# Pacing the first group's scattered rows by TensorE's progress, with the order of work searched anew

## The chip, the cores and the metric

The kernel runs on one core of one Trainium2 chip. Its metric is device time in microseconds (us). Each run is one execution of the whole program; the median of three runs of the kernel before is 510.87 us.

## The reference

The input is `x` of 8 batches x 512 tokens x 128 features, float32. Three steps add to it:

```
x = x + 0.5 * ffn(layernorm(x))
x = x + attention(layernorm(x))
x = x + 0.5 * ffn(layernorm(x))
```

`ffn` is a mixture of experts. A shared expert (128 to 2 x 256 to 128, silu(gate) * up) works on every token. Of 8 routed experts of the same size, each token goes to the two with the highest `sigmoid(x @ router.T + bias)`; their outputs are weighted by these scores over their sum. `attention` is linear attention with 8 heads of 16: q and k are rotated by position, k and v are summed over the 512 tokens into a 16 x 16 matrix a head, numerators and denominators come from q, a 5-tap convolution of v is added, the sum is multiplied by a gate and projected. It needs a whole batch at a time; the experts don't care for batches.

## The kernel before

**Tiles.** A batch is 4 tiles of 128 tokens. Routed rows are sorted by expert through DRAM. The batches form groups: (0,2), (2,5), (5,8) in the first `ffn` (called 1), and (0,2), (2,5), (5,7), (7,8) in the second (called 3). For a group, routing computes where each token's two copies go. GpSimd then writes them there by indirect DMAs: one **scatter** moves 128 rows of one tile for one of its two experts, so the first group has 2 x 8 = 16 scatters. SP loads the sorted rows two blocks of 128 at a time (a **pair**), TensorE transposes them, multiplies them by the expert that each block belongs to, and SP stores the result. When all of a group's pairs are stored, GpSimd fetches each token's two results back with indirect DMAs (a **gather**, 128 rows each), and VectorE adds them to `X`. There are 128 scatters and 128 gathers in all.

**Units.** A large product that fills a bank of PSUM is a **unit**: half of a batch's shared expert (S), a routed pair (R), or a third of a batch's attention projections (A). Each has one or two `front` halves. After the first half of a unit TensorE raises the semaphore `half_ready`, after the last `gu_ready`. ScalarE takes silu, VectorE multiplies (`hs`), TensorE multiplies down.

**The opening.** The weights come as float32; ScalarE and VectorE cut each expert's into a high and a low part (`cut_w`, `cut_w_lo`, line 1449 for VectorE) before the first routed pair may start. In the meantime the norms, the shared units of the first `ffn` and the routing of the first groups go on. SP first loads the inputs, then fills the DRAM rooms of the sorted rows with zeros. The first group's scatters need its places, its normalized rows and that fill.

**The order of work.** Every engine's queue is written out by the program `Plan`. It describes about a thousand operations with costs in units of 10 ns, what they need and when their results land. `schedule` simulates them as a list: each engine takes, of the operations that could start within 100 ns of the first, the one with the best rank. `search` runs it 600 times with randomly shifted ranks (seed 1) and keeps the order with the earliest end. The queue orders, the choice of buffers and the semaphore values all come from that one plan.

**The pace of moves.** Scatters and gathers are the **moves**. In `schedule` a move may start no sooner than `PACE` = 160 (1.6 us) after the start of the move before, as long as the last routed unit isn't done. Its own cost is 126. In the program, `pace` lets GpSimd wait before each move for TensorE's progress: `through` counts the unit halves that were finished in the plan when the move started, and GpSimd waits for that value of `half_ready` and `gu_ready`. Both don't hold for the scatters of the first group, which `paced` leaves out:

```
def paced(self, key):
    return key[:3] != ("scatter", *GROUP_LIST[0])
```

GpSimd's queue holds, besides the moves, only the 24 norm roots (`root`, line 1130); a root that stands behind a waiting move waits as well. SP's queue holds the loads, stores and outputs; `load` of a group's first pair waits for all of its scatters.

Of the kernel before, what the change touches and what calls it, by code (L numbers as in the profile page):

```python
# [34 lines left out]
GROUP_LIST = [(l, g) for l in (1, 3) for g in range(NG[l])]  # L35
# [38 lines left out]
class Plan:  # L74
# [275 lines left out]
    def schedule(self, rank):  # L350
        ops, end, start = self.ops, {}, {}
# [21 lines left out]
        def finish(key):  # L373
            for user in users.get(key, ()):
                missing[user] -= 1
                if missing[user] == 0:
                    admit(user)
# [59 lines left out]
        def settle(key, t):  # L437
            name = key[0]
            if name == "front" and (key[2] == 1 or (*key[0:2], 1) not in ops):
                self.units.append(key[1])  # L440
                if key[1][0] in "RS":
                    self.hidden.append(key[1])
            if name in count:
                count[name] += 1
            if name == "hidden_turn":
                ht[0] = ("hT_copy", key[1])
            if name == "sdown":
                ht[0] = ("add", key[1], key[2], "shared")
                self.shared_order.append(key[1:3])
            if name in self.HELD:  # L450
                i = min((i for i in range(2) if not bank[i] or after(bank[i]) is not None),
                        key=lambda i: after(bank[i]) if bank[i] else 0)
                self.misc[key], bank[i] = i, (self.HELD[name], *key[1:])
            if name == "hi":
                i = min((i for i in range(XT) if not xt[i] or after(xt[i]) is not None),
                        key=lambda i: after(xt[i]) if xt[i] else 0)
                l, b = key[1:]
                self.xt_before[l, b] = xt[i] and xt[i][1]
                self.xt_of[l, b] = i
                xt[i] = ("front", ("A", b, "VG") if l == 2 else ("S", l, b, 1), 0)  # L460
            if name == "gather" and key[3] == 0:
                i = min((i for i in range(YG) if not yg[i] or after(yg[i]) is not None),
                        key=lambda i: after(yg[i]) if yg[i] else 0)
                l, b = key[1:3]
                self.yg_before[l, b] = yg[i] and yg[i][1:3]
                self.yg_of[l, b], yg[i] = i, ("add", l, b, "second")
# [4 lines left out]
        last_routed = ("front", ("R", len(self.pair) - 1), 0)  # L471
        while waiting:
            near = {}
            for key in waiting:
                t = dynamic(key)
                if t is None:
                    continue
                engine = ops[key][0]
                t = max(t, ready_at[key], free[engine])
                if key[0] in ("scatter", "gather") and self.paced(key) and last_routed not in end:  # L480
                    t = max(t, last_move + PACE)
                near.setdefault(engine, []).append((t, key))
            best = None
            for engine, candidates in near.items():
                soon = min(t for t, _ in candidates) + NEAR
                t, key = min((c for c in candidates if c[0] <= soon),
                             key=lambda c: rank[c[1]])
                if best is None or t < best[0]:
                    best = (t, serial[key], key, engine, t)
            if not best:  # L490
                return False
            _, _, key, engine, t = best
            waiting.discard(key)
            settle(key, t)
            length = ops[key][1]
            if engine == "PE":
                if t - free[engine] > COLD and t > 1000:
                    cold = t + COLD
                length = length if t >= cold else 1.8 * length
            start[key], end[key] = t, t + length  # L500
            free[engine] = end[key]
            if key[0] in ("scatter", "gather"):
                last_move = t
            self.order[engine].append(key)
            finish(key)
        return True

    def paced(self, key):
        return key[:3] != ("scatter", *GROUP_LIST[0])

    def through(self, key):

        if not self.paced(key):
            return 0, 0
        t = self.start[key]
        return tuple(sum(1 for u in self.units if self.end.get(("front", u, j), t) + HOP <= t) for j in (1, 0))


def build(nc, x, wq, wqp, wk, wv, wg, wo, lepe_w, lepe_b, sgate, sup, sdown, gate_w, up_w, down_w,
# [8 lines left out]
    with ExitStack() as ctx:  # L528
# [596 lines left out]
        def _(pool):  # L1125
# [6 lines left out]
            def pace(*key):  # L1132

                half_through, through = plan.through(key)
                wait(once, half_ready, half_through)
                wait(once, gu_ready, through)
# [424 lines left out]
```

## Time and profile before

| | us |
|---|---|
| median of 3 runs (lowest to highest) | 510.87 (510.63 to 511.22) |
| profiled execution, span from the first to the last instruction | 540.9 |
| TensorE busy in it | 474.9 |
| VectorE busy | 348.5 |
| GpSimd busy | 282.4 |
| ScalarE busy | 272.3 |

The profile is of one execution; the page gives its span and no other time of it. Busy times are of that execution. In the page's second part each digit is the busy share of a fortieth of the span in tenths. In a timeline, the bracket at a line's end is the idle time of the engine before the instruction and what ended it: `issue` is time in which nothing shown was waited for, `remote` an origin outside the engines shown.

### The profile page before, as it was taken

Reading aid. Unit: us, or ns where it says so; the run is one execution under the profiler, and the core shown is the slowest. Engines: PE = TensorE matmul, PEld = TensorE weight load, DVE = VectorE, ACT = ScalarE, POOL = GpSimd, SP = SyncE. Lnnn points to the kernel's source line nnn. Section 1 sums busy time; section 2 is a strip of 40 time slices with the busy share of each in tenths; the row PEclk is TensorE's granted clock in tenths of the full one; section 3 lists DMA queues with packets and bytes.
Section 4 is the critical chain, followed back from the end, with each engine's and each line's share of the span. In section 5 each row is a group of like instructions: output and inputs, shape, how many; then the busy total and the mean of one; then the engine's idle time right before and its main releaser. Section 6 shows DMA issues by size and latency. Waiting matters only on the chain.

```text
span 540.9 us, 9674 instructions
## 1 busy us (share of the span) xinstructions
PE 474.9 (88%) x2975; PEld 381.7 (71%) x2975; DVE 348.5 (64%) x1064; ACT 272.3 (50%) x612; POOL 282.4 (52%) x290
## 2 busy tenths in 40 slices
PE   7894687998999999999999999999999998899980
PEld 3673676776777787777877777877777776667760
DVE  4992795322358765889996789998966224344442
ACT  5861232555566466647647556653554543443530
POOL 4167054545566506666715666776555545553543
PEclk9999799999999999999999999999999999999997
DMA  8961112234431223321132321113442433442222
GB/s 240 377 215 55 54 64 68 79 112 130 121 89 55 87 80 109 103 65 58 57 102 75 86 66 59 45 45 93 121 133 82 127 95 92 124 127 59 79 73 68
DMA packets 74352, 53.66 MB, mean 99 GB/s; under 512 B 9664, under 2 KB 68928, under 8 KB 74304
## 3 DMA queue, kind: packets, MB, share of 16 engines
q1 hardware_dynamic: 66112, 36.26, 22.4%
q0 software_dynamic: 8192, 16.79, 10.0%
q8 instruction: 26, 0.43, 0.3%
q14 instruction: 22, 0.18, 0.1%
HBM read 26.87 MB, written 26.15 MB: 98 GB/s over the span
## 4 chain that ended last, share of the span: by engine, by line
PE 53%; DVE 23%; issue 8%; ACT 7%; another core or an unknown queue 4%; DMA 2%; POOL 1%; SPq 1%; DVEq 0%; POOLq 0%; ACTq 0%
PE gu L881 15%; PE ht_ps L872 7%; PE gu L839 6%; PE gu L841 6%; PE gu L840 5%; PE xt_ps L822 3%; DVE hs L1219 2%; DVE hs L1215 2%; ACT gs L1025 2%; PE gu L799 2%; DVE raw L1415 2%; PE gu L801 1%; PE gu L800 1%; ACT xn L1048 1%
## 5 line engine op out<-in xcount | busy, mean ns | idle before, releaser
L1172 POOL DMA_INDIRECT yg<-y_sorted,places x128 | 123.0, 961 | 113.2 <-PE gu L841 72.4
L1151 POOL DMA_INDIRECT x_sorted<-xn,places x128 | 129.9, 1015 | 97.3 <-PE gu L841 36.2
L881 PEld LDWEIGHTS gu<-w,hT 128*128 128x128 f32 x708 | 87.1, 191 | 36.0 <-issue 33.7
L881 PE MATMUL gu<-w,hT 128*128 x708 | 100.3, 284 | 11.3 <-ACT hT L1031 6.7
L1025 ACT ACTIVATE gs<-gu 128x512 f32<-128x512 f32 x124 | 72.2, 583 | 53.5 <-PE gu L801 19.4
L1215 DVE TENSOR_TENSOR hs<-gs,gu 128x512 f32<-128x512 f32 x92 | 60.7, 662 | 49.6 <-ACT gs L1025 27.0
L839 PE MATMUL gu<-w,xbt_hi 128*128 x177 | 83.6, 473 | 7.1 <-ACT ys L1006 2.9
L1031 ACT ACTIVATE hT<-ht_ps 128x512 f32<-128x512 f32 x92 | 53.3, 580 | 56.6 <-PE ht_ps L872 38.8
L1201 DVE TENSOR_TENSOR xbt_lo<-xt_ps,xbt_hi 128x256 fp32r<-128x256 f32 x92 | 37.7, 410 | 64.9 <-ACT xbt_hi L1014 56.5
L841 PE MATMUL gu<-w,xbt_hi 128*128 x177 | 70.7, 399 | 0.0
L840 PE MATMUL gu<-w,xbt_lo 128*128 x177 | 70.2, 397 | 0.0
L1006 ACT ACTIVATE ys<-gu 128x256 f32<-128x256 f32 x92 | 34.4, 375 | 54.3 <-PE gu L881 41.0
L872 PE MATMUL ht_ps<-squares_sb,hs 128*128 128x128 f32 x354 | 55.5, 278 | 4.6 <-DVE hs L1215 3.5
L872 PEld LDWEIGHTS ht_ps<-squares_sb,hs 128*128 128x128 f32 x354 | 40.9, 141 | 18.7 <-DVE hs L1215 10.7
L1014 ACT ACTIVATE xbt_hi<-xt_ps 128x256 fp32r<-128x256 f32 x92 | 34.4, 373 | 27.8 <-PE gu L841 14.4
L1130 POOL TENSOR_TENSOR rstd<-ve,minus_half 128x4 f32<-128x4 f32 x24 | 26.8, 1116 | 40.0 <-DVE ve L1259 38.4
L1048 ACT ACTIVATE xn<-X,shifts,rstd 128x128 f32<-128x128 f32 x96 | 40.8, 486 | 13.3 <-DVE shifts L1263 10.1
L839 PEld LDWEIGHTS gu<-w,xbt_hi 128*128 128x128 f32 x177 | 33.8, 191 | 15.3 <-issue 13.1
L1238 DVE SCALAR_TENSOR_TENSOR X<-yg,wsel,X 128x128 f32<-128x128 f32 x128 | 36.4, 346 | 7.0 <-DMA yg<-y_sorted,places 6.5
L1219 DVE TENSOR_TENSOR hs<-gs,gu 128x512 f32<-128x512 f32 x32 | 21.8, 682 | 28.1 <-ACT gs L1025 25.7
L841 PEld LDWEIGHTS gu<-w,xbt_hi 128*128 128x128 f32 x177 | 33.6, 190 | 7.8
L822 PE MATMUL xt_ps<-squares_sb,xb 128*128 128x128 f32 x177 | 35.1, 277 | 4.2 <-DVE xbt_lo L1201 2.9
(132 smaller groups left out, 799.4 us busy)
## 6 DMA issues: line engine op xcount, KB each, us to landing
xb<-x_sorted SPq DMA_DIRECT2D x85, 128.0 KB
y_sorted<-ys SPq DMA_DIRECT2D x85, 128.0 KB
x_sorted<-yg SPq DMA_DIRECT2D x6, 512.0 KB, 5.7
X<-x_dram SPq DMA_DIRECT2D x8, 256.0 KB, 4.8
x_sorted<-xn,places POOLq DMA_INDIRECT x128
yg<-y_sorted,places POOLq DMA_INDIRECT x128
out_dram<-X SPq DMA_DIRECT2D x8, 256.0 KB
raw<-gate_w_dram SPq DMA_DIRECT2D x4, 256.0 KB, 4.3
```

What stands on the lines that cost most here:

```text
L822: mm = pe.transpose(xt_ps[:, j * P:(j + 1) * P], xb[r % XB][:, j], ident)
L839: pe.matmul(dst[:, j], xbt_hi[r % 2][:, at], hi, start=True, stop=False)
L840: pe.matmul(dst[:, j], xbt_lo[r % 2][:, at], hi, start=False, stop=False)
L841: mm = pe.matmul(dst[:, j], xbt_hi[r % 2][:, at], lo, start=False, stop=True)
L872: mm = pe.transpose(ht_ps[:, q * P:(q + 1) * P], hs[n % HB][:, q * P:(q + 1) * P], ident)
L881: mm = pe.matmul(dst[:, j * D:(j + 1) * D], hT[r % 2][:, at:at + P], w_flat[:, bass.ds(expert[r][j] + 2 * GU + half * D, D)], start=half = ...
L1025: nc.scalar.activation(dst, src, ACT.Silu).then_inc(silu_done, 1)
L1031: nc.scalar.activation(hT[r % 2][:, 0:n], ht_ps[:, 0:n], ACT.Copy).then_inc(hT_done, 1)
L1048: ins = nc.scalar.activation(xn[:, b, t], X[:, b, t], ACT.Identity, bias=shifts[:, l, b, t:t + 1], scale=rstd[:, l, b, t:t + 1])
L1151: nc.gpsimd.indirect_dma_start(x_sorted[l, g], bass.IndirectOffsetOnAxis(places[l, g][:, k, t:t + 1], 0), xn[:, b, t % T], None).then_inc( ...
L1172: nc.gpsimd.indirect_dma_start(yg[slot][:, k, t], None, y_sorted[l, g], bass.IndirectOffsetOnAxis(places[l, g][:, k, at:at + 1], 0)).then_ ...
L1215: v.tensor_tensor(hs[n % HB][:].rearrange("p (j i) -> p j i", j=2)[:, 0:k], gs[n % GB][:].rearrange("p (j i) -> p j i", j=2)[:, 0:k], bank ...
```

## The change

The exception for the first group is taken out. In the plan its 16 scatters too lie at least 1.6 us after the move before, and in the program GpSimd waits before each of them for TensorE's progress. Since the plan's search runs over the changed rule, the whole order of work, on every engine, may come out another. No operation is added or removed.

```diff
-                if key[0] in ("scatter", "gather") and self.paced(key) and last_routed not in end:
+                if key[0] in ("scatter", "gather") and last_routed not in end:
                     t = max(t, last_move + PACE)
...
-    def paced(self, key):
-        return key[:3] != ("scatter", *GROUP_LIST[0])
-
     def through(self, key):
-
-        if not self.paced(key):
-            return 0, 0
         t = self.start[key]
         return tuple(sum(1 for u in self.units if self.end.get(("front", u, j), t) + HOP <= t) for j in (1, 0))
```

## Rows read from the trace of the kernel before

**Rows 1.** The page: span, busy time of engines, TensorE and its granted clock by slices.

```profile
span 540.9 us, 9674 instructions
...
PE 474.9 (88%) x2975; PEld 381.7 (71%) x2975; DVE 348.5 (64%) x1064; ACT 272.3 (50%) x612; POOL 282.4 (52%) x290
...
PE   7894687998999999999999999999999998899980
...
PEclk9999799999999999999999999999999999999997
```

**Rows 2.** Stretches: length, busy us of each engine (instructions), clock, DMA share, GB/s.

```profile
57.16:78.73 21.57, 19.52 (x124) 16.82 (x124) 20.63 (x61) 6.01 (x13) 6.02 (x6) 0.89 0.17 54
...
57.91:61.89 3.98, 3.98 (x10) 3.13 (x10) 3.67 (x13) 0.80 (x2) 0.00 (x0) 0.51 0.28 81
...
200.00:300.00 100.00, 95.43 (x624) 78.94 (x622) 79.98 (x243) 60.73 (x139) 57.41 (x56) 1.00 0.28 82
300.00:400.00 100.00, 93.49 (x615) 77.88 (x614) 88.84 (x275) 53.72 (x121) 65.51 (x64) 1.00 0.25 75
```

**Rows 3.** Timeline of GpSimd, then of SP: start, us, line, operation, idle before.

```profile
31.89 1.17 POOL L1151 DMA_INDIRECT x_sorted<-xn,places  x1 [0.20 <-issue]
33.10 2.03 POOL L1130 TENSOR_TENSOR rstd<-ve,minus_half 128x4 f32<-128x4 f32 x2
...
53.07 0.96 POOL L1151 DMA_INDIRECT x_sorted<-xn,places  x1 [0.30 <-issue]
69.01 0.96 POOL L1151 DMA_INDIRECT x_sorted<-xn,places  x1 [14.98 <-DVE places L1379]
...
55.32 2.43 SPq L729 DMA_DIRECT2D xb<-x_sorted  x5
...
116.09 3.20 SPq L729 DMA_DIRECT2D xb<-x_sorted  x4
```

**Rows 4.** Timeline of VectorE: the first instruction after each of three waits.

```profile
43.84 0.19 DVE L1280 TENSOR_TENSOR L<-misc,tables_sb 128x32 f32<-128x32 f32 x1 [2.20 <-remote]
...
57.16 0.69 DVE L1219 TENSOR_TENSOR hs<-gs,gu 128x512 f32<-128x512 f32 x1 [10.50 <-ACT gs L1025]
...
89.15 0.17 DVE L1358 TENSOR_SCALAR padded<-misc 128x8 int32<-128x8 f32 x1 [3.45 <-remote]
```

**Rows 5.** Timeline of ScalarE.

```profile
56.53 0.60 ACT L1025 ACTIVATE gs<-gu 128x512 f32<-128x512 f32 x1 [11.42 <-remote]
...
90.58 0.60 ACT L1031 ACTIVATE hT<-ht_ps 128x512 f32<-128x512 f32 x1 [3.86 <-remote]
```

**Rows 6.** Timeline of TensorE: shared units start at L799, transposes of loaded rows at L822.

```profile
41.11 0.48 PE L799 MATMUL gu<-xt_hi,sw_hi 128*128 128x512 f32 x1
...
44.79 0.47 PE L799 MATMUL gu<-xt_hi,sw_hi 128*128 128x512 f32 x1
...
57.91 0.80 PE L799 MATMUL gu<-xt_hi,sw_hi 128*128 128x512 f32 x1 [6.62 <-DVE hs L1219]
...
73.69 0.38 PE L822 MATMUL xt_ps<-squares_sb,xb 128*128 128x128 f32 x2
...
76.70 0.48 PE L799 MATMUL gu<-xt_hi,sw_hi 128*128 128x512 f32 x1
```

**Rows 7.** Waits from 28 to 66 us: us in total, times, longest.

```profile
PE ht_ps L892 <- issue: 2.7, 2, 1.7
```

**Rows 8.** Timeline of GpSimd in the second group's scatters.

```profile
83.45 0.99 POOL L1151 DMA_INDIRECT x_sorted<-xn,places  x1 [1.35 <-PE gu L841]
...
88.53 0.96 POOL L1151 DMA_INDIRECT x_sorted<-xn,places  x1 [0.30 <-issue]
```

**Rows 9.** DMA queues from 40 to 48 us, then from 48 to 56.

```profile
q8 instruction: 1, 0.02, 0.7%
...
q0 software_dynamic: 192, 0.39, 12.4%
```

## The prediction

> **What bounds the kernel now.** I read the page first. Its second part shows TensorE at nine tenths nearly everywhere, with one deep dent in the fourth slice (a slice is 13.5 us), where its granted clock dips as well [rows 1]. The table of stretches gives the rest: TensorE is busy 95.43 of 100 us in the middle of the run and 93.49 in the next hundred [rows 2]. So TensorE bounds all but the opening, and what is gained in the opening is kept, as long as the routed work that follows can start earlier.
>
> GpSimd's timeline says what runs in the dent. The 16 scatters of the first group go out between 31.89 and 54.03 us: one, two norm roots, then 15 in a row, 0.96 us of work and 0.30 us between them [rows 3]. The other three engines' timelines show a hole beside it. VectorE stands 2.20 us before 43.84 and 10.50 us before 57.16 [rows 4]. ScalarE stands 11.42 us before 56.53, and the profile names none of this core's engines as the releaser [rows 5]. TensorE halts twice, 2.7 us together, inside one set of 16 matmuls (L892) that needs nothing new in between [rows 7], and then stands 6.62 us before 57.91 [rows 6]. So the hole is no wait that the program wrote. It starts about 11 us into the run of scatters and ends when the last one has landed: SP's first load of sorted rows, which waits for all 16, goes out at 55.32, ScalarE resumes at 56.53 [rows 3, 5].
>
> Which engine's time in the opening counts is read from the stretch after the hole: from 57.16 to 78.73, where the first routed matmul starts, VectorE is busy 20.63 of 21.57 us [rows 2]. The opening is VectorE's chain (routing of the second group, cutting the expert weights, the shared units), so the hole's price is VectorE's: 2.20 + 10.50 = 12.70 us. The half clock behind the hole (0.51 granted, the 1.2 GHz level, after TensorE had stood for 6.62 us) fits ten matmuls into 3.98 us, where the full clock would need about half of that [rows 2]; VectorE is busy 3.67 of those 3.98 us, so I count it at nothing and keep half, 2.0 us, as the bound.
>
> **The change part by part.**
> (1) The 16 scatters get waits on `half_ready` and `gu_ready`: each starts when TensorE has finished as many units as it had in the plan. Nothing is added to GpSimd's work. A wait already met costs nothing to see: a paced scatter whose wait was met starts 0.30 us after the one before, as an unpaced one does (88.53 and 53.07 [rows 3, 8]).
> (2) In the plan, moves now lie at least 1.6 us apart. 16 scatters then begin over 15 x 1.6 = 24.0 us, where before it was 53.07 - 31.89 = 21.2 us. Of the last one's start to the first load 2.25 us pass (53.07 to 55.32 [rows 3]). So the first load goes out at 31.89 + 24.0 + 2.25 = 58.1 in place of 55.32, if TensorE keeps to the plan. Who waits: SP's queue (five loads stand behind it), then TensorE's first transposes of rows at 73.69 [rows 6]. If the hole's 12.70 us go, these are wanted at 61.0: from 58.1 plus 2 us of landing (estimate: the scatters' own 2.25) that is just in time. So this costs nothing in the likeliest case, with less than one us of cover left; its upper bound is in the third rival.
> (3) Behind a waiting scatter stand the norm roots of later batches (two at 33.10, after the first scatter [rows 3]). A scatter that waited one unit would hold them: two neighbouring units start 3.7 us apart here (41.11 and 44.79 [rows 6]). The plan knows of that order, so I take 0; the bounds are 0 and one such step, 3.7 us.
> (4) What the pace takes away: a burst that runs on while TensorE stands. With it, when TensorE is held, GpSimd stops too. I take it that the long hole goes. It won't go wholly: under the same pace, the second group has five scatters at 1.26 us from 83.45 to 89.5 (TensorE was ahead), and there ScalarE stands 3.86 us and VectorE 3.45 us, again with no releaser named [rows 4, 5, 8]. So I leave one such hole of 3.5 us in the account: 12.7 - 3.5 = 9.2 us gained. Bounds: 12.7 + 2.0 = 14.7 us (all of it and the clock), and 0 (the paced scatters bunch as those did).
> (5) The second group's first scatter starts at 69.01, released by its places [rows 3]; 12.7 us earlier, at 56.3, it would find the first group's last one still out until about 57. That holds 24 scatters back by a us, and their rows are first loaded at 116.09 [rows 3], long after: nothing.
> (6) The order of all work is searched anew, some 600 random trials over the same costs. No row prices another order. Two hundreds of this kernel with the same kind of work differ by 95.43 - 93.49 = 1.9 us of TensorE's idle time [rows 2]; over 4.6 such hundreds, were each to differ at random, about 4 us. I take 0, and 4 us either way as the bound.
>
> **From the profile to the runs.** The sum in the profiled execution: 540.9 - 9.2 = 531.7 us. The page gives that execution its span alone, and it is 30.0 us over the 510.87 us median of the runs. TensorE's idle time in it is 540.9 - 474.9 = 66.0 us [rows 1]. The added 30 us must lie in such idle time for the most part, since matmul steps are at full clock outside the holes (granted 0.98 in the mean). If all of it lies there and evenly, 36/66 = 0.55 of any hole stands in an undisturbed run. So I forecast 0.55 x 9.2 = 5.1 us: **505.8 us**, faster. The ends are 0 (the hole is the profiled execution's alone) and 9.2 (it is whole).
>
> The Trainium skill (Runtime: NRT & Kernel Launch, "Instruction fetch mechanics") says that an engine draws its instructions in blocks through a DMA queue of its own while it works on the block before, mostly unseen. The trace bears that out at the hole: one instruction packet between 40 and 48 us, none between 48 and 56, where the software queue's packets took 12.4% of the DMA engines' time [rows 9]. So neither late instructions nor full DMA engines are the visible cause, and a cause that isn't the burst's would leave the hole where it is: by that the time stays 510.9, the first rival.
>
> **The rivals.**
> *No gain: the hole isn't the scatters' doing, or is mostly the profiled execution's.* For it: no DMA load and no releaser in the hole, and the scatters run for 10 us (from 31.89 to 41.6) before VectorE is held [rows 3, 4, 9]; the 30 us between span and median. Against: the hole ends with the scatters. Worth 0 +/- 4 us from the new order: 510.9, from 507 to 515.
> *Partial bunching.* The plan's units run late on the chip, so the waits are met when reached, and the scatters bunch as at 83.45. Then one or two holes of 3.5 to 7 us stay: 0.55 x (12.7 - 7) = 3.1 us, 507.7. It has the forecast's sign and is part of its range.
> *Slower: the first group's rows come late.* The last scatter may hang on the last shared units. The six shared units left then start from 57.91 to 76.70, 3.8 us apart, at VectorE's pace [rows 6]. Without the hole the last starts at 76.70 - 12.7 = 64.0; a scatter freed at its end, 65.5, is loaded at 67.7 and in at 69.8, and TensorE wanted the rows at 61.0: 8.8 us in which it has no shared unit left to do. That price is real in every run, the hole perhaps not. It decides from the point where the delay is more than what the hole was worth in the runs (0 to 9.2 us). With the hole worth nothing and half the price paid: 510.87 + 4.4 = 515.3 us; with all of it 519.7.
>
> **How the numbers follow.** Forecast with partial bunching 0.45, time 501 to 509.5. No gain 0.23. Late rows 0.32, of which nearly all slower. About 0.2% (1 us) is what a measurement of this kernel can tell from no change. Faster: 0.45 + 0.06 (a lucky order in the second case) = 0.51. Same: 0.12. Slower: 0.05 + 0.32 = 0.37. Range: the low end is 9.2 whole and 1.5 us of luck in the order, 500; the high end takes in the rival's middle, 515.5. As cases of both signs are likely, the forecast's own range is 501 to 509.5.
>
> **What would show it.** Right: in the profile after, the fourth slice of TensorE, VectorE and ScalarE loses its dent, no wait over 4 us without a releaser stands before 60 us, the granted clock stays at full there, the first routed matmul starts near 78.7 - 9.2 = 69.5 us, and later stretches keep their 93 to 95% of TensorE. Step 2 is wrong if TensorE's first transposes of rows wait for the load. Step 4 is wrong if the 16 scatters still run at 1.26 us beside a hole, or run spaced and the hole is there. The third rival shows as waits of GpSimd's first-group scatters on the late shared units, and TensorE idle before its first routed unit. If the profiled span falls by 9 us and the median doesn't, the hole was the profile's.

## The result, and the profile after

The change makes the kernel slower where it was timed: 518.39 us median (518.11 to 519.9, four runs) against 510.75 (510.27 to 511.22, four runs), a ratio of 1.0159 with a 95% interval of 1.0141 to 1.0177. The forecast was 505.8, faster. Ratios here and below compare only fast executions with fast ones on the same chip, so a ratio can differ a little from that of the medians beside it.

One fact has to come first, since no number below can be read without it. The kernel before was timed on six occasions, and its medians fall into two groups. On two of them, the timing of the change among them, it takes 510.6 to 510.8 us. On the four others it takes 538.6 to 542.7, each time on another chip. I speak of 511 chips and 540 chips after that. In the experiments no chip was used on two occasions, so it isn't shown whether the group goes with the chip or with something else about the occasion. The rows ahead of the prediction ([rows 1] to [rows 9]) are from one execution that by its span of 540.9 belongs to the second kind, while the times beside them were from the first kind. The profile after is from a 511 chip. Its execution took 518.11 us at a span of 516.1: recording adds nothing that is seen here, and the two us are what lies around the span.

The page of the changed kernel (busy time, TensorE, VectorE and granted clock by slices of 12.9 us):

```profile
span 516.1 us, 9677 instructions
...
PE 472.0 (91%) x2975; PEld 382.6 (74%) x2975; DVE 348.6 (68%) x1064; ACT 275.2 (53%) x612; POOL 283.4 (55%) x290
...
PE   8899959999999999999999999999999989998980
...
DVE  4999963332678856999995999999875234442442
...
PEclk9999979999999999999999999999999998999996
```

The dent of [rows 1] is gone from slice four, as forecast, and a smaller one stands in slice six (64.5 to 77.4 us), with the dip of the clock. The timelines of the engines in that place, first TensorE (L816 transposes loaded rows, L833 is a routed unit's first product), then VectorE (L1443 cuts an expert's weights, L1195 takes the low part of a loaded pair's rows, L1373 ends a group's routing), then GpSimd and SP:

```profile
63.70 0.38 PE L816 MATMUL xt_ps<-squares_sb,xb 128*128 128x128 f32 x2
...
66.19 2.02 PE L886 MATMUL ht_ps<-swd,hs 128*128 128x128 f32 x16 [2.11 <-DVE X L1222]
...
69.82 0.41 PE L816 MATMUL xt_ps<-squares_sb,xb 128*128 128x128 f32 x2 [0.88 <-DVE xbt_lo L1195]
73.33 0.79 PE L833 MATMUL gu<-w,xbt_hi 128*128 x1 [3.10 <-DVE w L1443]
...
61.26 0.63 DVE L1443 TENSOR_TENSOR w<-raw,w 128x512 fp32r<-128x512 f32 x1
...
67.58 0.41 DVE L1195 TENSOR_TENSOR xbt_lo<-xt_ps,xbt_hi 128x256 fp32r<-128x256 f32 x1
...
69.26 0.41 DVE L1195 TENSOR_TENSOR xbt_lo<-xt_ps,xbt_hi 128x256 fp32r<-128x256 f32 x1
...
72.42 0.18 DVE L1373 CAST places<-spot_f 128x24 int32<-128x24 f32 x1
72.51 0.69 DVE L1443 TENSOR_TENSOR w<-raw,w 128x512 fp32r<-128x512 f32 x1
...
32.47 1.17 POOL L1145 DMA_INDIRECT x_sorted<-xn,places  x1 [13.18 <-PE gu L795]
...
58.81 1.29 POOL L1145 DMA_INDIRECT x_sorted<-xn,places  x1 [0.30 <-issue]
...
61.39 9.23 SPq L723 DMA_DIRECT2D xb<-x_sorted  x8
```

The reader is to see three things. The first group's last scatter starts at 58.81 and the first load goes out at 61.39. The rows are in, and TensorE transposes them from 63.70 on. The first routed product still starts only at 73.33, and what it waits for last, for 3.10 us, is the last expert's weights: VectorE cuts them at 72.51, directly behind the end of the third group's routing at 72.42. TensorE stands 2.11 and 0.88 us before that as well, each time for VectorE. Nothing asks for that routing so early: the third group's scatters start at 105 us. The order is the plan's. Later stretches are as full as [rows 2] or fuller (columns as there; those of the old plan on a 511 chip, in `waits_only_2` below, are fuller still, with TensorE at 97.04 and 96.64):

```profile
200.00:300.00 100.00, 96.66 (x649) 80.69 (x648) 89.64 (x285) 63.91 (x146) 59.67 (x59) 1.00 0.28 80
300.00:400.00 100.00, 96.27 (x619) 79.89 (x618) 85.58 (x265) 54.59 (x122) 66.23 (x65) 1.00 0.28 86
```

### The profile page after: what moved, and what is told of

Same layout as the page of the kernel before. It is cut to its first block, busy times and chain, and to the rows that moved or that the text cites. A ratio compares the mean times of both kernels' runs of the same rounds, so it can differ in the third digit from the quotient of the medians.

```text
span 516.1 us, 9677 instructions
## 1 busy us (share of the span) xinstructions
PE 472.0 (91%) x2975; PEld 382.6 (74%) x2975; DVE 348.6 (68%) x1064; ACT 275.2 (53%) x612; POOL 283.4 (55%) x290
## 4 chain that ended last, share of the span: by engine, by line
PE 59%; DVE 24%; issue 7%; ACT 5%; POOL 2%; DMA 2%; SPq 1%; POOLq 0%; DVEq 0%; ACTq 0%
PE gu L875 16%; PE gu L833 8%; PE ht_ps L866 8%; PE gu L835 7%; PE gu L834 7%; PE xt_ps L816 3%; DVE hs L1213 3%; PE gu L793 2%; PE gu L795 2%; PE gu L794 2%; DVE hs L1209 2%; DVE raw L1409 1%; DVE X L1232 1%; DVE X L1222 1%; DVE stats L1243 1%
## 5 line engine op out<-in xcount | busy, mean ns | idle before, releaser
L1145 POOL DMA_INDIRECT x_sorted<-xn,places x128 | 129.8, 1014 | 89.2 <-PE gu L835 34.9
L875 PEld LDWEIGHTS gu<-w,hT 128*128 128x128 f32 x708 | 88.3, 192 | 26.8 <-issue 24.0
L1209 DVE TENSOR_TENSOR hs<-gs,gu 128x512 f32<-128x512 f32 x92 | 60.8, 662 | 60.9 <-ACT gs L1019 55.6
L833 PE MATMUL gu<-w,xbt_hi 128*128 x177 | 84.2, 476 | 7.5 <-DVE w L1443 3.1
L1195 DVE TENSOR_TENSOR xbt_lo<-xt_ps,xbt_hi 128x256 fp32r<-128x256 f32 x92 | 37.7, 410 | 54.0 <-ACT xbt_hi L1008 53.8
L833 PEld LDWEIGHTS gu<-w,xbt_hi 128*128 128x128 f32 x177 | 34.1, 193 | 16.0 <-issue 13.0
L816 PE MATMUL xt_ps<-squares_sb,xb 128*128 128x128 f32 x177 | 34.9, 276 | 3.3 <-DVE xbt_lo L1195 3.1
L886 PE MATMUL ht_ps<-swd,hs 128*128 128x128 f32 x256 | 31.9, 278 | 5.4 <-DVE X L1222 5.4
```

The costliest lines, as they stand in the source:

```text
L816: mm = pe.transpose(xt_ps[:, j * P:(j + 1) * P], xb[r % XB][:, j], ident)
L833: pe.matmul(dst[:, j], xbt_hi[r % 2][:, at], hi, start=True, stop=False)
L875: mm = pe.matmul(dst[:, j * D:(j + 1) * D], hT[r % 2][:, at:at + P], w_flat[:, bass.ds(expert[r][j] + 2 * GU + half * D, D)], start=half = ...
L1145: nc.gpsimd.indirect_dma_start(x_sorted[l, g], bass.IndirectOffsetOnAxis(places[l, g][:, k, t:t + 1], 0), xn[:, b, t % T], None).then_inc( ...
L1209: v.tensor_tensor(hs[n % HB][:].rearrange("p (j i) -> p j i", j=2)[:, 0:k], gs[n % GB][:].rearrange("p (j i) -> p j i", j=2)[:, 0:k], bank ...
```

## The experiments

Two of the runs stand below for the two plans on one chip: `waits_only_2` has the plan of before with the first group's waits added, and `after_again` is the changed kernel. The ratio in each row is to the kernel before on the same chip. A label with `_2` or `_3` is the same kernel on another chip.

| run | plan's own end | kernel before there | this | ratio (95%) |
|---|---|---|---|---|
| before_again | 501.8 | 540.2 | 540.3 | 1.0027 (0.9981 to 1.0074) |
| waits_only | 501.8 | 540.2 | 535.1 | 0.9919 (0.9880 to 0.9957) |
| no_waits | 506.2 | 540.2 | 543.6 | 1.0113 (1.0052 to 1.0174) |
| ranks_held | 513.7 | 540.2 | 549.0 | 1.0193 (1.0123 to 1.0262) |
| after_again | 506.2 | **510.6** | 517.7 | 1.0151 (1.0122 to 1.0180) |
| waits_only_2 | 501.8 | **510.6** | 510.8 | 1.0001 (0.9991 to 1.0011) |
| no_waits_2 | 506.2 | **510.6** | 518.8 | 1.0155 (1.0136 to 1.0174) |
| ranks_held_2 | 513.7 | **510.6** | 522.3 | 1.0231 (1.0214 to 1.0248) |
| before_seed9 | 511.3 | 541.1 | 550.6 | 1.0162 (1.0092 to 1.0232) |
| after_seed9 | 508.1 | 541.1 | 540.0 | 0.9973 (0.9937 to 1.0009) |
| before_long | 489.0 | 541.1 | 533.5 | 0.9869 (0.9794 to 0.9945) |
| after_long | 497.4 | 541.1 | 533.1 | 0.9839 (0.9771 to 0.9906) |
| before_seed9_2 | 511.3 | 538.6 | 549.6 | 1.0289 (1.0171 to 1.0406) |
| after_seed9_2 | 508.1 | 538.6 | 538.2 | 1.0073 (1.0024 to 1.0121) |
| before_long_2 | 489.0 | 538.6 | 535.8 | 0.9888 (0.9764 to 1.0013) |
| after_long_2 | 497.4 | 538.6 | 535.4 | 1.0014 (0.9964 to 1.0063) |
| before_seed9_3 | 511.3 | 542.7 | 547.7 | 1.0141 (1.0052 to 1.0229) |
| after_again_2 | 506.2 | 542.7 | 533.6 | 0.9874 (0.9804 to 0.9944) |

All times are medians in us. The plan's own end is the figure that `schedule` gives for the order that it kept.

**Is the hole the program's, or that one execution's?** `before_again` is the kernel before, unchanged.

> The kernel before, unchanged, for a second profiled execution. If the hole of 10 to 12 us near 45 to 57 us belonged to the one profiled execution (its span was 30 us over the median), this one's span lies within 2 to 3 us of its time (508 to 509 us against 510.8) and no wait over 4 us without a releaser stands before 60 us. If the hole is the program's, it is there again and the span is well over the median.

Its span came out at 535.5, with the time of that execution 537.3. So the recording doesn't lengthen the span; here every run is long, none of the ten under 534.7. Of its waits from 28 to 66 us (us in total, times, longest), those without a releaser on this core:

```profile
ACT gs L1025 <- remote: 7.2, 1, 7.2
DVE hs L1219 <- issue: 6.3, 1, 6.3
...
ACT xt_hi L1000 <- remote: 2.9, 1, 2.9
...
DVE L L1280 <- remote: 1.9, 1, 1.9
```

The hole is there again, with single waits of 6 to 7 us where they were 10 to 12 [rows 4, 5]. It isn't one execution's: it comes again with the program on a 540 chip.

**Do the waits cost time?** The old plan, with the waits added in the program alone:

```diff
     def through(self, key):
 
-        if not self.paced(key):
-            return 0, 0
         t = self.start[key]
```

> The plan of before to the last instruction, but GpSimd waits before each of the first group's 16 scatters for TensorE's progress as that plan has it. Theory A (the loss of 7.6 us is in the plan: later first rows and another order of work): the waits alone cost nothing, 510.8 +/- 1. Theory B (the waits hold scatters, roots and first rows back on the chip): 515 to 519.

> The plan of before with the waits of the first group added in the program alone. Where before takes 540 it was 535.1. Theory A (the loss is in the plan): where before takes 510.8, the same within 1 us, 510 to 512. Theory B (the waits delay rows and roots): 514 to 519.

On the 511 chip 510.76 against 510.62: the waits are free. GpSimd's timeline there shows why (L1149 are the scatters, L1128 norm roots):

```profile
32.35 1.17 POOL L1149 DMA_INDIRECT x_sorted<-xn,places  x1 [0.97 <-PE gu L799]
33.56 2.03 POOL L1128 TENSOR_TENSOR rstd<-ve,minus_half 128x4 f32<-128x4 f32 x2
...
49.00 1.04 POOL L1149 DMA_INDIRECT x_sorted<-xn,places  x1 [0.31 <-PE gu L799]
...
54.13 0.96 POOL L1149 DMA_INDIRECT x_sorted<-xn,places  x1 [0.30 <-issue]
```

All but the first are met when they are reached or within 0.2 us of it; the last scatter starts at 54.13, where it was 53.07 on the 540 chip without waits [rows 3]. On the 540 chip the same edit gained 5.1 us (0.9919). So it does something where the hole is, and nothing where it isn't. It doesn't do it by spacing the scatters out: but for one pause they still follow each other at about 1.3 us. GpSimd's timeline there, and then waits of that chip from 28 to 66 us:

```profile
43.77 1.01 POOL L1149 DMA_INDIRECT x_sorted<-xn,places  x1 [0.30 <-issue]
46.70 0.96 POOL L1149 DMA_INDIRECT x_sorted<-xn,places  x1 [1.92 <-remote]
47.97 0.96 POOL L1149 DMA_INDIRECT x_sorted<-xn,places  x1 [0.30 <-issue]
```

```profile
DVE padded L1356 <- remote: 3.3, 1, 3.3
...
ACT xt_hi L998 <- remote: 2.2, 1, 2.2
POOL x_sorted L1149 <- remote: 1.9, 1, 1.9
```

The third line is that pause. No wait of ScalarE or VectorE without a releaser is over 3.3 us there, so the hole is cut short and not gone.

**Does the new plan cost time?** The changed kernel without the first group's waits:

```diff
     def through(self, key):
+        if key[:3] == ("scatter", *GROUP_LIST[0]):
+            return 0, 0
         t = self.start[key]
```

> The changed kernel's plan to the last instruction, without the waits before the first group's scatters. Theory A: it stays at 518.4 +/- 1. Theory B: it falls back to 511 to 514.

> The changed kernel's plan without the first group's waits. Where before takes 510.8: theory A 518.4 +/- 1, theory B 511 to 514. Where before takes 540: 543.6 again, and the changed kernel with its waits is 3 to 6 us under it if the waits are what takes the hole away.

On the 511 chip it stays at 518.75, beside 517.70 with the waits. With `waits_only_2` that settles it for this kind of chip: the loss of 7 us is wholly in the plan. `no_waits_2` is also the one profile on a 511 chip with the first group's scatters unpaced: no wait without a releaser is over 1.0 us there from 28 to 66 us. The changed kernel itself beside them:

> The changed kernel again, beside the three edits below on one chip. The call before ran where the kernel before takes 540.2 us; it had taken 510.8 where the change was timed. If this call finds the 510.8 of before: 518.4. If it finds the 540: there the unpaced burst has a hole (7 to 11 us without a releaser on ScalarE), which the pace should take away; so the loss of 7.6 us shrinks to 2 to 5 us, 542 to 545, against theory A without that hole, 548.

Busy time by stretches (PE, PEld, DVE, ACT, POOL, then clock, DMA share and GB/s), first of `waits_only_2`, the old plan:

```profile
45.00:60.00 15.00, 13.80 (x91) 12.38 (x90) 13.31 (x42) 2.39 (x4) 9.18 (x10) 0.89 0.25 83
60.00:75.00 15.00, 13.95 (x98) 11.43 (x97) 13.39 (x43) 5.24 (x12) 9.59 (x10) 1.00 0.25 81
75.00:90.00 15.00, 14.77 (x96) 12.12 (x96) 6.66 (x18) 8.39 (x18) 8.61 (x9) 1.00 0.33 107
```

and of `after_again`, the new one, on the same chip:

```profile
45.00:60.00 15.00, 13.94 (x96) 11.56 (x95) 14.48 (x41) 5.12 (x10) 8.91 (x9) 1.00 0.09 36
60.00:75.00 15.00, 8.83 (x64) 7.50 (x63) 12.12 (x43) 2.30 (x6) 8.03 (x8) 0.91 0.36 110
75.00:90.00 15.00, 14.84 (x84) 12.00 (x82) 4.32 (x9) 7.80 (x17) 7.71 (x9) 0.87 0.29 93
```

TensorE is busy 13.95 - 8.83 = 5.1 us less in the stretch from 60 to 75. In the next it is as busy, but at a granted clock of 0.87 it gets 84 matmuls done where the old plan has 96; the old plan has its own dip earlier (0.89). Each busy time multiplied with its clock and summed gives 12.3 + 14.0 + 14.8 = 41.0 us for the old plan and 13.9 + 8.0 + 12.9 = 34.9 for the new. These 6.1 us are more than the 5.0 us between the spans of the same two executions (515.0 and 510.0; their medians are 6.9 apart), so the loss lies in these 45 us, and the rest of the run gives a little back. The old plan's first routed product, and the last weights cut ahead of it:

```profile
62.36 0.38 PE L820 MATMUL xt_ps<-squares_sb,xb 128*128 128x128 f32 x2
...
66.70 0.49 PE L837 MATMUL gu<-w,xbt_hi 128*128 x1
```

```profile
63.40 0.63 DVE L1447 TENSOR_TENSOR w<-raw,w 128x512 fp32r<-128x512 f32 x1
63.94 0.41 DVE L1199 TENSOR_TENSOR xbt_lo<-xt_ps,xbt_hi 128x256 fp32r<-128x256 f32 x1
```

The same places in `after_again`:

```profile
67.26 0.42 DVE L1195 TENSOR_TENSOR xbt_lo<-xt_ps,xbt_hi 128x256 fp32r<-128x256 f32 x1
...
72.19 0.68 DVE L1443 TENSOR_TENSOR w<-raw,w 128x512 fp32r<-128x512 f32 x1
...
73.01 0.79 PE L833 MATMUL gu<-w,xbt_hi 128*128 x1 [3.11 <-DVE w L1443]
```

TensorE takes the first rows at 62.36 there and at 63.29 in `after_again`, 0.9 us later; VectorE starts on the low part of that first pair's rows at 63.94 and at 67.26, 3.3 us later. The last weights are cut at 63.40 there and at 72.19, 8.8 us later, and the first routed product starts 6.3 us later. The wait for the weights is 3.1 us of that. The rest is the same engine: TensorE stands 2.2 and 0.9 us for an add and a low part that lie between the steps of the third group's routing. The plans agree with the chip in this: they have the first routed product at 64.3 and at 71.1. Asked alone, with no chip, the kernel's planner says what the one cut is worth: with the last cut ranked ahead of the third group's routing and all other ranks of the changed kernel held, it puts the first routed product at 68.1 in place of 71.1, but its own end at 505.2 in place of 506.2. So by the planner the late cut makes 3 us of the delay and only about 1 us of the whole; this order wasn't run.

**The rule, or the new search?** The new rule applied once to the ranks that the old rule's search had found:

```diff
-                if key[0] in ("scatter", "gather") and self.paced(key) and last_routed not in end:
+                if key[0] in ("scatter", "gather") and (self.all_paced or self.paced(key)) and last_routed not in end:
...
+        self.all_paced = True
         self.schedule(best[1])
```

> The search runs with the old rule and finds the ranks of before; the last schedule is then made once with the new rule, so the 16 scatters are paced in plan and program but nothing is searched anew. The plan's own end goes from 501.8 to 513.7 us. If the rule makes the loss and the new search took part of it back, this is slower than the changed kernel: 521 to 526 us. If the new search made the loss (a worse draw), this is nearer to before: 511 to 515.

> The ranks that the old rule's search found, scheduled once with the new rule; the plan's end is 513.7 us against 501.8 before and 506.2 changed. Where before takes 510.8: 521 to 526 us if the rule itself makes the loss and the new search took part back; 511 to 515 if the draw of the search made it. Where before takes 540 it was 549.0.

On the 511 chip as expected: 522.25 is 11.6 us over before, and the plan says 11.9. On the 540 chip it was 549.0, 8.7 over before there. So the order of before doesn't stand the rule, and the new search won back 4.6 of the 11.6. But this doesn't mean that all orders lose by it. The order of before was tuned by 600 trials to the old rule. The plan's own ends for other seeds of the search, 600 trials each, worked out by the kernel's own planner:

```
seed          1     2     3     4     5     6     7     8     9    10    11   mean
old rule  501.8 508.1 510.4 511.4 509.3 510.2 503.2 508.3 511.3 509.8 506.8   508.2
new rule  506.2 510.9 511.5 511.4 511.3 511.2 511.5 510.0 508.1 512.3 509.3   510.3
```

By these the rule costs 2.1 us in the mean, where the ends have a standard deviation of 3.2 (old) and 1.8 (new); seed 1, which both kernels use, is the best of eleven under either rule. I took seed 9, where the new rule has the better plan:

```diff
-ROUNDS, SEED = 600, 1
+ROUNDS, SEED = 600, 9
```

> The kernel before with its search started from seed 9 in place of 1: the old rule, another draw, 600 trials as before. Its plan ends at 511.3 us (before: 501.8). The three plans timed on one chip came out 8.6 to 11.5 us over their plan's end. Theory A1 (the draw of the order makes the loss): 520 to 523. Theory A2 (the rule of the pace makes it, whatever the draw): near 511.

> The changed kernel with seed 9. Its plan ends at 508.1, under that of the old rule with the same seed. A1: 517 to 520, faster than before_seed9, so that the sign of the change turns with the seed. A2: 5 to 8 us slower than before_seed9.

> Old rule, seed 9 (plan's end 511.3), again, since the call before ran where the kernel before takes 541 us and plans come out 39 us over their end. Where it takes 510.6: A1 520 to 523, A2 near 511. Where it takes 541: 550 again.

> New rule, seed 9 (plan's end 508.1). Where before takes 510.6: A1 517 to 520, by 2 to 4 us faster than the old rule with this seed; A2 slower than it by 5 to 8. Where before takes 541: 540 again.

> Old rule, seed 9. Where before takes 510.6: A1 (the draw) 520 to 523, at least as slow as the changed kernel without any pace on the first group; A2 (the rule) near 511. Where before takes 540: 550 a third time.

All of these were timed on 540 chips. There the sign of the change does turn: with seed 9 the paced kernel is 10.6 and 11.4 us faster than the unpaced one. Only 3.2 of that is in the planner's ends. The rest fits the hole, but isn't shown to be it, since no run adds the waits alone to the plan of this seed. The unpaced kernel has a still longer hole with it (`before_seed9_2`, waits from 28 to 66 us):

```profile
ACT xt_hi L1000 <- remote: 13.6, 1, 13.6
PEld misc L934 <- issue: 10.3, 2, 10.1
DVE X L1228 <- remote: 10.3, 1, 10.3
```

So seed 9 doesn't part the draw from the rule on a 511 chip, which is where the question was. It stays open.

**Longer searches.** The best ranks of each kernel, carried on for 5000 trials more; the ranks found are written into the kernel, and the search does one round:

```diff
-ROUNDS, SEED = 600, 1
+ROUNDS, SEED = 1, 1
+SHIFT = {
+    ...
+}
...
-        best, shift = None, {}
+        best, shift = None, {families[i]: v for i, v in SHIFT.items()}
```

> The old rule, and the search of before carried on for 5000 further trials from its own best ranks (the ranks found are written into the kernel; plan's end 489.0). If the plan's end carries over to the chip, 498 to 501 and faster than both kernels by over 2%. If a search overfits its own costs, the offset grows and it is 503 to 510.

> The new rule, and the search of the changed kernel carried on likewise (plan's end 497.4, under the 501.8 of before). A1: 506 to 509, faster than the kernel before although all 16 scatters are paced. A2: over 512.

> Old rule, longer search (plan's end 489.0). Where before takes 510.6: 498 to 501 if the plan's gain of 12.8 us is kept, 503 to 510 if part of it is an overfit to the plan's costs (where before takes 541 it kept 7.6 of 12.8).

> New rule, longer search (plan's end 497.4, between 489.0 and the 501.8 of before). Where before takes 510.6: 506 to 509 by A1, so faster than the kernel before with all scatters paced; over 512 by A2. Where before takes 541: 533 again, level with the old rule's longer search though its plan is 8.4 us longer, if the pace gives something back there.

Both are faster than the kernel before on the first chip (0.9869 and 0.9839) and not clearly on the second (0.9888 and 1.0014, intervals that hold 1). The plan's gains over the kernel before of 12.8 and 4.4 us don't show in that proportion: on a 540 chip both land at 533 to 536. Whether they keep more on a 511 chip wasn't measured.

**The change on a 540 chip.**

> The changed kernel. Where before takes 510.6: 518 a third time. Where before takes 540 it hasn't been timed: its plan without the waits took 543.6 there, so 538 to 541 if the waits take as much off as they took off the plan of before (5.1 us), 543.6 if they do nothing in this order.

533.62 against 542.65, ratio 0.9874 (0.9804 to 0.9944), on one chip and in four runs: here the change is **faster**, by more than expected. Among its waits from 28 to 66 us none without a releaser is over 1.5 us long, and `no_waits`, the same plan with the scatters at full rate, has two long ones:

```profile
DVE padded L1354 <- remote: 8.1, 1, 8.1
ACT gs L1021 <- remote: 6.6, 1, 6.6
```

TensorE waits for the late weights here too, even longer (first routed product at 76.80):

```profile
76.80 0.79 PE L833 MATMUL gu<-w,xbt_hi 128*128 x1 [6.00 <-DVE w L1443]
```

## Why the prediction was wrong, point by point

**What bounds the kernel** was read rightly for a 540 chip, except that the granted clock of [rows 1] dips in the fifth slice and not in the fourth: the hole and VectorE's chain behind it were there again. On the 511 chips, where the times were, the hole isn't there, but VectorE's chain is: in `waits_only_2` VectorE is busy 13.31 and 13.39 of 15 us from 45 to 75 us, in `after_again` 14.48 and 12.12. What the forecast gained was the hole, and what the result lost was the order of that chain.

**Step 1, the waits cost nothing: right,** 510.76 against 510.62.

**Step 2, first rows out in time: right by its own sign, with the time off.** Forecast 58.1 for the first load, measured 61.39; TensorE's transposes follow at 63.7, and no wait for the load stands there. Of the 3.3 us over the forecast, 0.6 are a later first scatter (32.47), 2.3 that the sixteen take 26.3 us from first to last in place of 24.0, and 0.3 the step to the load. The new plan had it so: the planner's own time of that load is 61.7, against 57.2 in the old plan.

**Step 3, roots behind scatters: nothing was seen of it.** Three roots now stand between single scatters (33.7 to 39.4 us), each released as soon as the scatter before it is out, and in `after_again` TensorE waits for no norm longer than 0.3 us.

**Step 4, the hole goes: right in kind, on a 540 chip.** The dent is gone in the changed kernel (`after_again_2`, no such wait over 1.5 us). The waits alone left 3.3 us of it and gained 5.1 us, where 9.2 had been taken for the profiled execution.

**"From the profile to the runs": the first failed step.** It set the 30.0 us between the span and the median down to idle time evenly spread and kept 0.55 of the hole, 5.1 us. The runs showed the hole whole on one kind of chip and, where the times were, nothing to gain: the waits alone give 510.76 against 510.62 there. The rival "no gain" held this and had 0.23. There was a sign in the trace of before: over the whole run, and not only in the hole, it has waits of ScalarE and VectorE named `issue`. Compare the same kernel on the two kinds, `waits_only` (us in total, times, longest):

```profile
DVE hs L1213 <- issue: 18.6, 9, 2.7
ACT hT L1029 <- issue: 8.6, 8, 2.9
```

In `waits_only_2`, the identical program, neither ScalarE nor VectorE has one such row. A span that is 30 us over the median speaks of another chip or other conditions than those of the times, and a step that turns on it should have been a rival with its own number, not a factor.

**Step 6, the order searched anew: the second failed step, and the one that made the loss.** It was taken at 0 within 4 us, from two stretches of one order. It was 7 us. The error is in the reasoning as much as in the size. Two stretches of one order say nothing of another order, while the planner's own ends, which need no chip, were to be had: 501.8 and 506.2, a loss of 4.4. And with the old rule seed 1 gives the best end of eleven seeds, 501.8 where the mean is 508.2; a search over a changed rule had more room to come out worse than better.

**The third rival** had the right sign and the right symptom, a first routed unit 6.3 us late with TensorE idle before it, and a price of 8.8 at most (519.7). That the time lies within its price is luck, as its mechanism was another: no engine waits for the load of the first rows. TensorE waits for what VectorE makes of them and for the last weights, which VectorE's order has among and behind the steps of the third group's routing, and no scatter of that group starts before 105 us. Why the search kept that order is not shown; that moving that one cut forward would win the time back wasn't tried, and the planner gives it about 1 us of the 7.

What the Trainium skill says of instruction fetch (Runtime: NRT & Kernel Launch, "Instruction fetch mechanics") decided nothing. The rival that hung on it came true as far as the gain goes, but the runs show it so because the hole was absent where the times were; on the 540 chip the scatters' waits did shorten it.

What holds the engines in the hole stays open. What the runs show is when it comes: on a 540 chip in a run of scatters (`no_waits`, 8.1 us), and not in the same run of scatters on a 511 chip (`no_waits_2`, nothing over 1.0 us).

## What to carry to other kernels

Hold a profile's span against the times before anything else: when the two differ by more than what lies around a span, the profile is of another chip or of other conditions, and its waits may not be in the times. Where a planner searches the order, an edit to one of its rules is two edits; part them by keeping the old order and adding the rule's effect alone, ask the planner for its own end first, and where the old order was a lucky draw, expect a new one to lose some of that luck. After a re-search, look for the last thing that the first big stage waits for, since a planner that ends within a few us of its best may have put it anywhere.

## What the runs showed of the hardware that I had not expected

The same program takes 510.8 us on one chip and 535.1 on another (`waits_only`, 4.8%), at nearly the same granted clock (0.988 and 0.992). ScalarE and VectorE are held on the second, again and again for up to 3 us, with no releaser that the profile shows; the longest such halts, 6 to 14 us in the kernels without waits, come while GpSimd issues indirect DMAs in a row. Letting these wait for TensorE's progress is worth 0.8% there and nothing on the first.
